# Pair 31's transposes: from TensorE to VectorE's 32x32 blocks, in a graph-attention kernel

## The chip, the cores and the metric

One core of one Trainium2 chip. The metric is the device time of one execution in microseconds. Before the change it is 289.98 us, the median of 3 runs (289.61 to 290.26).

## What is computed

Two graph layers with a residual and a layer norm each, over 64 graphs of 128 nodes and 256 features:

```python
# layer 0, for each graph
q, k = split(X @ Wqk);  v = X @ Wv
agg = adj @ (k * mask)
w   = mask * (q * agg).sum(-1) / 16          # one weight per node
x1  = layernorm(X + softmax(w over nodes)[:, None] * v)
# layer 1, for each graph
query, key, value = x1 @ Wq.T + bq, x1 @ Wk.T + bk, x1 @ Wv.T + bv
e   = adj * exp(query @ key.T)
out = layernorm(x1 + (e / e.sum(-1)) @ value)
```

## The kernel before

Two graphs make a pair; there are 32 pairs, 0 to 31. A slot t of the program works on several pairs at once: it projects pair t+2 and forms its node weights and their softmax, it finishes x1 of pair t+1, it runs layer 1's queries, values and scores for pair t, and it attends and stores for pair t-1 and before. Every engine runs its own queue in the order in which the code lists it, with semaphores between the queues. The slots run from -2 to 29; slot 29 (`DRAIN`, PAIRS - 3) is the last one, and each engine then has a hand-written `drain()` for what is left of pairs 29, 30 and 31. There pair 30 is called `a` and pair 31 `b`.

The softmax over the nodes needs the node weights as a row. VectorE writes them as two columns, `w_col` (128 nodes by 2 graphs), so they have to be transposed into rows, and the softmax's result transposed back into the columns `p_col`, by which VectorE scales the projected values in `sum_x1` (L656). There are two ways, and `by_tensor(pair)` (L30) chooses:

- By TensorE (pairs 0, 1, 2 and 31). `transpose_w` of TensorE (L995) writes the rows to PSUM, VectorE takes their maximum (`row_max`, L818), ScalarE the exponentials and their sum (L597), VectorE inverts the sum (`invert_sum`, L814) and scales the row into `p_row` (L907), TensorE transposes it (`transpose_p`, L1001), and VectorE copies two columns of the result to `p_col` (L660).
- By VectorE (pairs 3 to 30). `transpose_w` of VectorE transposes `w_col` in four blocks of 32x32 (L809), the maximum and the exponentials follow, ScalarE scales the row (`scale_row`, L493) between the two halves of the z copy (L485), and VectorE transposes that row back in four blocks (L912).

Around the change, in slot 29 and behind it: VectorE's `attended` part computes x2 of pair 28 in two halves (L883) and takes its statistics (L646), the first instruction of VectorE's `drain()` is `x1t_lo_a`, the low part of pair 30's transposed x1 (L732), and `sum_x1(31)` (L665) stands behind it. From there runs x1 of pair 31: statistics (L646), variance (L744), the root on GpSimd (L317), the norm on VectorE (L694), TensorE's transposes of x1 (L1076). TensorE's queries and values of pair 30 stand between its score matmuls (L1050) and L1076; the first of them wait for `x1t_lo_a`.

Of the kernel before, what the change touches and what calls it, by code (L numbers as in the profile page):

```python
# [13 lines left out]
PAIRS = GRAPHS // 2  # L14
# [10 lines left out]
FIRST, DRAIN = -2, PAIRS - 3  # L25
# [3 lines left out]

def by_tensor(pair):  # L30

    return pair < 3 or pair == PAIRS - 1


def exists(pair):

    return not isinstance(pair, int) or 0 <= pair < PAIRS


def build(nc, x_pairs, xt_pairs, adjt_pairs, params0, params1, value_bias, out_pairs):  # L40
    ctx = ExitStack()
    with ctx:  # L42
# [140 lines left out]
        def graph(g, width=DIM):  # L183
            return slice(g * width, (g + 1) * width)
# [21 lines left out]
        def w_rows(r):  # L206
            return w_row_ps(r) if by_tensor(r) else w_row[0:2, :]
# [4 lines left out]
        def p_full_ps(r):  # L212
            return yv_ps(r)[:, 1, 0:NODES]
# [230 lines left out]
        def _(act):  # L444
# [94 lines left out]
            def slot(t, r):  # L539
# [59 lines left out]
                if exists(t) and r != 0:  # L599
                    act.wait_ge(z_done, t + 1)  # L600
                    bias_half(z, 0, z_half_copied)
                    if exists(t + 2) and not by_tensor(r + 2):
                        scale_row(t + 2, r + 2)
                    bias_half(z, 1, z_copied)
# [337 lines left out]
        def _(pe):  # L942
# [5 lines left out]
            def split_product(out, parts):  # L948

                for n, (s_hi, s_lo, m_hi, m_lo) in enumerate(parts):  # L950
                    mm = split_half(out, s_hi, s_lo, m_hi, m_lo, n == 0, n == len(parts) - 1)
                return mm

            def aggregate(u, r):

                if r < SPLIT:
                    pe.wait_ge(adjm_done, u + 1)
                    pe.wait_ge(x_loaded[r % 4], transfers4(u, r))
                else:
                    pe.wait_ge(adjm_lo_done, u + 1 - SPLIT)  # L960
                    pe.wait_ge(x_lo_done, u + 1 - SPLIT)
                if exists(u - 1):
                    pe.wait_ge(agg_copied, u)
                for g in range(2):
                    n = graph(g, NODES)
                    if r < SPLIT:
                        mm = nc.tensor.matmul(agg_ps[:, g, :], adjm[r % 2][:, n], x_raw[r % 4][:, graph(g)],  # L967
                                              start=True, stop=True)
                    else:
                        mm = split_product(agg_ps[:, g, :], [(adjm_hi[r % 2][:, n], adjm_lo[r % 2][:, n],  # L970
                                                              x_hi[r % 2][:, graph(g)], x_lo[r % 2][:, graph(g)])])
                mm.then_inc(agg_done, 1)
# [6 lines left out]
            def project(u, r, g):  # L979

                if g == 0:
                    pe.wait_ge(xt_lo_done, u)
                if exists(u - 1) and r > 1:
                    pe.wait_ge(x1_sum_done[g], 1 if r == 2 else u)
                for k in range(HALVES):
                    mm = project_half(u, r, g, k)
                    if r == 2 and g == 0 and k == HALVES - 1:
                        transpose_p(1, 1)
                mm.then_inc(yv_done[g], 1)

            def transpose_w(u, r):

                for g in range(2):
                    pe.wait_ge(w_done[g], u + 1)
                nc.tensor.transpose(w_row_ps(r), w_col[:, 0:2], ident[:, :]).then_inc(w_row_done, 1)  # L995

            def transpose_p(u, r):

                pe.wait_ge(ident_ready, 1)
                pe.wait_ge(p_row_done, u + 1)  # L1000
                nc.tensor.transpose(p_full_ps(r), p_row[:, :], ident[:, :]).then_inc(p_col_done, 1)  # L1001
# [19 lines left out]
            def transpose_x1(out, r):  # L1021
                for g in range(2):
                    if r == 0 and g == 1:
                        pe.wait_ge(x1_done, 1)
                    for k in range(HALVES):
                        c = g * DIM + k * 128
                        mm = nc.tensor.transpose(out[:, k, g, :], x1[r % 2][:, c:c + 128], ident[:, :])  # L1027
                mm.then_inc(x1t_done, 1)

            def queries(hi, lo, weighted=None):  # L1030
                for m in range(HALVES):
                    if m == 1 and weighted:
                        transpose_w(*weighted)
                    c = slice(m * 128, (m + 1) * 128)
                    mm = split_product(z_ps[:, m, :], [(
                        at_hi[:, k, c], at_lo[:, k, c], hi[:, k, :, :].rearrange("p g n -> p (g n)"),
                        lo[:, k, :, :].rearrange("p g n -> p (g n)")) for k in range(HALVES)])
                mm.then_inc(z_done, 1)

            def values(hi, lo, g):  # L1040
                return split_product(val_ps[:, g, 0:VAL_COLS], [(
                    hi[:, k, g, :], lo[:, k, g, :], wv1_hi[:, k, :], wv1_lo[:, k, :]) for k in range(HALVES)])

            def scores(u, out, zs, xs):
                pe.wait_ge(z_half_copied, u + 1)
                for k in range(HALVES):
                    if k == 1:
                        pe.wait_ge(z_copied, u + 1)
                    for g in range(2):
                        mm = nc.tensor.matmul(out[:, g, :], zs[:, k, graph(g, NODES)], xs[:, k, g, :],  # L1050
                                              start=(k == 0), stop=(k == HALVES - 1))
                mm.then_inc(score_done, 1)
# [57 lines left out]
            def transpose_next(t, r):  # L1110
                if r == -1:
                    pe.wait_ge(first_half_normed, 1)
                    pe.wait_ge(biases_ready, 1)
                else:
                    pe.wait_ge(x1_done, t + 2)
                    pe.wait_ge(z_copied, t + 1)
                transpose_x1(x1t_ps, r + 1)

            def slot(t, r):
                if exists(t + 2):  # L1120
                    if r > 0:
                        aggregate(t + 2, r + 2)
                    project(t + 2, r + 2, 0)
                if exists(t + 2):
                    project(t + 2, r + 2, 1)
                if exists(t - 1):

                    pe.wait_ge(edge_lo_done, t)
                    pe.wait_ge(val_lo_done, t)
                    for g in range(2):  # L1130
                        n = graph(g, NODES)
                        mm = split_product(sum_ps[:, g, 0:VAL_COLS], [(edge_hi[:, n], edge_lo[:, n],
                                                                       val_hi[:, g, :], val_lo[:, g, :])])
                    mm.then_inc(sum_done, 1)
                if exists(t):

                    pe.wait_ge(x1t_lo_done, t + 1)
                    if r == 0:
                        pe.wait_ge(at_lo_done, HALVES + 1)
                        pe.wait_ge(wv1_lo_done, 1)  # L1140
                        pe.wait_ge(biases_ready, 1)
                    queries(x1t_hi, x1t_lo, (t + 2, r + 2) if r > 0 and by_tensor(r + 2) else None)
                if r == DRAIN:
                    pe.wait_ge(x1_done, t + 2)
                    pe.wait_ge(agg_copied, PAIRS)
                    transpose_x1(x1t_drain_ps, r + 1)
                if exists(t):

                    values(x1t_hi, x1t_lo, 0)
                    if r == 0:  # L1150
                        transpose_w(2, 2)
                    values(x1t_hi, x1t_lo, 1).then_inc(val_done, 1)
                    if r == DRAIN:
                        transpose_p(t + 2, r + 2)

                    if exists(t - 1):
                        pe.wait_ge(x2_done, t)
                    else:
                        for g in range(2):
                            pe.wait_ge(x1_sum_done[g], 2)  # L1160
                    scores(t, score_ps, z, x1t)
                if r != DRAIN:
                    if by_tensor(r + 2):
                        transpose_p(t + 2, r + 2)
                    transpose_next(t, r)
# [39 lines left out]
            transpose_w(1, 1)  # L1205
            transpose_next(-1, -1)
            slots(pe, slot, 0)
            drain()

# [32 lines left out]
```

## Time and profile before

| | |
|---|---|
| median of 3 runs | 289.98 us |
| profiled execution | 290.11 us |
| its span, first to last instruction | 288.3 us |
| mean granted TensorE clock | 0.995 |
| TensorE busy | 281.0 us (97%) |
| VectorE busy | 250.2 us (87%) |
| ScalarE busy | 248.5 us (86%) |
| GpSimd busy | 216.3 us (75%) |

The profile is one execution. Its span is 1.8 us shorter than its time: what lies around the first and the last instruction. Slot 29 and the drain fill the stretch from about 261 us to the end. PE is TensorE's matmuls, PEld its weight loads, DVE VectorE, ACT ScalarE, POOL GpSimd. A matmul of PE is shown longer than the distance to the next one, since they are pipelined; starts tell the queue's pace better than durations.

### The profile page before, as it was taken

The page shows a single profiled execution, that of the slowest core. Times are in us where ns is not written, and L with a number is a line of the kernel's source. Part 1 is how long each engine was busy: PE and PEld are TensorE (multiplying, and loading weights), DVE is VectorE, ACT ScalarE, POOL GpSimd, SP SyncE. Part 2 cuts the span into 40 slices and gives each one's busy share as a digit, 9 for nine tenths or more (in the row PEclk, how much of TensorE's full clock was granted, in tenths as well). Part 3 has the DMA queues.
Part 4 walks back from the last instruction along what each step waited for, and adds up shares of the span by engine and source line. Part 5 has one row for each costly group of instructions (what it writes and reads, how often), then busy time and mean ns, then how long its engine had stood idle before and what let it go on. Part 6 is the DMA issues. An engine that isn't in the chain of part 4 may idle for free.

```text
span 288.3 us, 7134 instructions
## 1 busy us (share of the span) xinstructions
PE 281.0 (97%) x1956; PEld 261.6 (91%) x1956; DVE 250.2 (87%) x841; ACT 248.5 (86%) x625; POOL 216.3 (75%) x269
## 2 busy tenths in 40 slices
PE   8999999999999999999999999999999999999991
PEld 7889999999999999999999999999999999999990
DVE  1588999999899999998999998999999989999775
ACT  3445889999999999999999999999999999998763
POOL 1546988788898888789887888988887898877332
PEclk9999999999999999999999999999999999999997
DMA  6930234232344323334433333434233334210112
GB/s 231 338 107 38 91 95 116 89 110 94 111 129 127 118 87 104 98 102 127 127 102 100 108 97 103 127 127 118 89 103 96 105 127 127 91 54 28 48 39 110
DMA packets 19166, 31.27 MB, mean 108 GB/s; under 512 B 2128, under 2 KB 6608, under 8 KB 19152
## 3 DMA queue, kind: packets, MB, share of 16 engines
q1 hardware_dynamic: 19152, 31.11, 35.0%
q8 instruction: 6, 0.10, 0.1%
q14 instruction: 8, 0.07, 0.1%
HBM read 22.71 MB, written 8.39 MB: 108 GB/s over the span
## 4 chain that ended last, share of the span: by engine, by line
PE 94%; DMA 2%; DVE 1%; issue 1%; ACT 0%; POOL 0%; SPq 0%; POOLq 0%; DVEq 0%; ACTq 0%
PE ps L944 25%; PE ps L945 25%; PE ps L946 25%; PE ps L1050 10%; PE ps L1027 5%; DMA p<-params 2%; PE ps L967 1%; PE ps L1183 1%; PE ps L1055 1%; PE ps L1006 1%; PE ps L1190 0%; DVE x L684 0%; POOLq L42 0%; POOL rstd L317 0%; PE ps L1012 0%
## 5 line engine op out<-in xcount | busy, mean ns | idle before, releaser
L944 PE MATMUL ps<-w_hi,xt_hi 128*128 128x512 f32 x124 | 49.1, 396 | 0.0
L945 PE MATMUL ps<-w_lo,xt_hi 128*128 128x512 f32 x124 | 48.6, 392 | 0.0
L946 PE MATMUL ps<-w_hi,xt_lo 128*128 128x512 f32 x124 | 48.5, 391 | 0.0
L377 POOL TENSOR_TENSOR edge_lo<-edge,edge_hi 128x256 fp32r<-128x256 f32 x29 | 21.5, 741 | 32.3 <-ACT edge_hi L558 32.3
L310 POOL TENSOR_TENSOR x1b<-x,bv_all 128x512 f32<-128x512 f32 x31 | 39.9, 1289 | 3.0 <-DVE x L883 2.1
L364 POOL TENSOR_TENSOR xt_lo<-xt_raw,xt_hi 128x512 fp32r<-128x512 f32 x30 | 38.4, 1281 | 1.6 <-ACT xt_hi L450 1.6
L388 POOL TENSOR_TENSOR rstd<-var_eps,minus_half 128x4 f32<-128x4 f32 x31 | 31.6, 1019 | 9.3 <-DVE var_eps L855 9.2
L371 POOL TENSOR_TENSOR x_lo<-x_raw,x_hi 128x512 fp32r<-128x512 f32 x28 | 36.2, 1294 | 0.0
L944 PE MATMUL ps<-wv_hi,x1t_hi 128*128 128x258 f32 x124 | 35.7, 288 | 0.0
L640 DVE CUSTOM_DVE_ANT_0 agg<-ps,agg,adjt 128x256 f32<-128x256 f32 x64 | 30.4, 479 | 5.6 <-issue 3.8
L946 PE MATMUL ps<-wv_hi,x1t_lo 128*128 128x258 f32 x124 | 35.2, 284 | 0.0
L945 PE MATMUL ps<-wv_lo,x1t_hi 128*128 128x258 f32 x124 | 35.2, 284 | 0.0
L944 PE MATMUL ps<-x1t_hi,at_hi 128*128 128x256 f32 x124 | 35.2, 284 | 0.0
L945 PE MATMUL ps<-x1t_lo,at_hi 128*128 128x256 f32 x124 | 34.9, 282 | 0.0
L946 PE MATMUL ps<-x1t_hi,at_lo 128*128 128x256 f32 x124 | 34.8, 280 | 0.0
L468 ACT ACTIVATE x<-x,shift,rstd 128x256 f32<-128x256 f32 x62 | 34.2, 605 | 0.3 <-POOL shift L322 0.3
L468 ACT ACTIVATE x<-x_sum,shift,rstd 128x256 f32<-128x256 f32 x58 | 31.7, 594 | 2.4 <-POOL shift L391 2.4
L1050 PE MATMUL ps<-x1t,z 128*128 128x128 f32 x240 | 31.7, 275 | 0.0
L665 DVE SCALAR_TENSOR_TENSOR x_sum<-ps,p_col,x_raw 128x256 f32<-128x256 f32 x64 | 28.0, 480 | 2.8
L485 ACT ACTIVATE z<-ps,z_bias 128x256 f32<-128x256 f32 x62 | 27.7, 453 | 2.5 <-PE ps L946 2.5
L883 DVE SCALAR_TENSOR_TENSOR x<-ps,den_inv,x1b 128x256 f32<-128x256 f32 x58 | 26.8, 468 | 3.5
L1050 PEld LDWEIGHTS ps<-x1t,z 128*128 128x128 f32 x240 | 29.6, 192 | 0.0
(173 smaller groups left out, 912.1 us busy)
## 6 DMA issues: line engine op xcount, KB each, us to landing
xt_raw<-xt_pairs SPq DMA_DIRECT2D x32, 256.0 KB, 2.7
x_raw<-x_pairs SPq DMA_DIRECT2D x32, 256.0 KB, 2.7
out_pairs<-x SPq DMA_DIRECT2D x31, 256.0 KB, 2.0
adjt<-adjt_pairs SPq DMA_DIRECT2D x32, 129.0 KB, 2.1
p<-params SPq DMA_DIRECT2D x1, 770.0 KB, 6.6
p<-params SPq DMA_DIRECT2D x1, 512.0 KB, 3.8
p<-params SPq DMA_DIRECT2D x1, 256.0 KB, 4.8
out_pairs<-x SPq DMA_DIRECT2D x2, 128.0 KB, 1.8
```

What stands on the lines that cost most here:

```text
L310: nc.gpsimd.tensor_tensor(to[:, :].rearrange("p (g d) -> p g d", g=2), x1[r % 2][:, :].rearrange("p (g d) -> p g d", g=2), bv_all[:, :].un ...
L364: nc.gpsimd.tensor_tensor(xt_lo[r % 2][:, :, :, :].rearrange("p t g n -> p (t g n)"), xt_raw[r % 2][:, :], xt_hi[r % 2][:, :, :, :].rearra ...
L371: nc.gpsimd.tensor_tensor(x_lo[r % 2][:, :], x_raw[r % 4][:, :], x_hi[r % 2][:, :].bitcast(F32), ALU.subtract).then_inc(x_lo_done, 1)
L388: nc.gpsimd.tensor_tensor(rstd[r % 2][:, :, :], var_eps[:, :, :], minus_half[:, :, :], ALU.pow)\
L468: last = nc.scalar.activation(out[:, graph(g)], in_[:, graph(g)], ACT.Identity, bias=shift[r % 2][:, layer, g:g + 1], scale=rstd[r % 2][:, ...
L485: nc.scalar.activation(to[:, m, :], z_ps[:, m, :], ACT.Identity, bias=z_bias[:, m:m + 1]).then_inc(done, 1)
L640: nc.vector.tensor_tensor_reduce(agg[:, g, :], y_ps(r)[:, g, :], agg[:, g, :], adjt[r % 4][:, PAIR_N + g:PAIR_N + g + 1], 0.0, ALU.mult, A ...
L665: nc.vector.scalar_tensor_tensor(out=x1_sum[r % 2][:, graph(g)], in0=v0_ps(r)[:, g, :], scalar=p_col[:, g:g + 1], in1=x_raw[r % 4][:, grap ...
L944: nc.tensor.matmul(out, s_hi, m_hi, start=first, stop=False)
L945: nc.tensor.matmul(out, s_hi, m_lo, start=False, stop=False)
L946: return nc.tensor.matmul(out, s_lo, m_hi, start=False, stop=last)
L1050: mm = nc.tensor.matmul(out[:, g, :], zs[:, k, graph(g, NODES)], xs[:, k, g, :], start=(k == 0), stop=(k == HALVES - 1))
```

## The change

`by_tensor` is true for pairs 0, 1 and 2 alone, and TensorE's `transpose_p` in slot 29 is gone; its `transpose_w` of that slot goes by the same condition. Pair 31 so takes the way of pairs 3 to 30.

```diff
 def by_tensor(pair):
-    return pair < 3 or pair == PAIRS - 1
+    return pair < 3
...
                     values(x1t_hi, x1t_lo, 1).then_inc(val_done, 1)
-                    if r == DRAIN:
-                        transpose_p(t + 2, r + 2)
```

In VectorE's queue, slot 29, from the second accumulator read of pair 31's weights (`w_col`) on; `x_0` is x2 of pair 28:

```order
 L640 ISA w_col 128x1
-L872 RECIPROCAL den_inv<-ps 128x2
-L883 SCALAR_TENSOR_TENSOR x_0<-ps,den_inv,x1b 128x256
-L818 TENSOR_REDUCE neg_max<-ps 2x1
+L809 STREAM_TRANSPOSE w_row<-w_col 32x32 x4
+L818 TENSOR_REDUCE neg_max<-w_row 2x1
+L872 RECIPROCAL den_inv<-ps 128x2
+L883 SCALAR_TENSOR_TENSOR x_0<-ps,den_inv,x1b 128x256
+L814 RECIPROCAL inv_sum<-exp_sum 2x1
 L883 SCALAR_TENSOR_TENSOR x_0<-ps,den_inv,x1b 128x256
```

Four block transposes come in, the maximum moves ahead of the first half of x2, and the inversion of the sum ahead of its second half.

Next in the same queue, to `sum_x1(31)`, across the border between the slot and the drain:

```order
 L646 BN_STATS stats<-x_0 128x6
-L814 RECIPROCAL inv_sum<-exp_sum 2x1
-L907 TENSOR_SCALAR p_row<-ps,inv_sum 2x128
+L912 STREAM_TRANSPOSE p_col<-ps 32x32 x4
 L732 TENSOR_TENSOR x1t_lo_a<-ps,x1t_hi_a 128x512
-L660 COPY p_col<-ps 128x2
 L665 SCALAR_TENSOR_TENSOR x_sum<-ps,p_col,x_raw 128x256 x2
```

Three short instructions go, and four block transposes stand ahead of `x1t_lo_a`.

In ScalarE's queue, slot 29, between the norm of pair 30 and the high part of its transposed x1:

```order
-L597 ACTIVATE ps,exp_sum<-ps,neg_max 2x128
-L485 ACTIVATE z<-ps,z_bias 128x256 x2
+L597 ACTIVATE ps,exp_sum<-w_row,neg_max 2x128
+L485 ACTIVATE z<-ps,z_bias 128x256
+L493 ACTIVATE ps<-ps,inv_sum 2x128
+L485 ACTIVATE z<-ps,z_bias 128x256
 L607 CAST x1t_hi_a<-ps 128x512
```

The row scaling stands between the two halves of the z copy. TensorE's queue loses one L995 and one L1001 and nothing in it moves; GpSimd's and the DMA queue keep their order.

## Rows read from the trace of the kernel before

**Rows 1.** The page's chain that ended last, shares of the span by engine.
```profile
PE 94%; DMA 2%; DVE 1%; issue 1%; ACT 0%; POOL 0%; SPq 0%; POOLq 0%; DVEq 0%; ACTq 0%
```

**Rows 2.** Timeline of weight loads: start us, duration us, engine, line, operation, [idle before].
```profile
269.70 0.14 PEld L1001 LDWEIGHTS ps<-ident,p_row 128*128 128x128 f32 x1
269.81 0.97 PEld L1050 LDWEIGHTS ps<-x1t,z 128*128 128x128 f32 x8
270.70 0.19 PEld L944 LDWEIGHTS ps<-x1t_hi_a,at_hi 128*128 128x128 f32 x1
...
273.45 0.19 PEld L946 LDWEIGHTS ps<-wv_hi,x1t_lo_a 128*128 128x128 f32 x1
273.79 0.46 PEld L1076 LDWEIGHTS ps<-ident,x 128*128 128x128 f32 x4 [0.16 <-issue]
```

**Rows 3.** Timeline of VectorE, slot 29 and the drain's start.
```profile
266.37 0.08 DVE L640 DVE_READ_ACCUMULATOR2_ANT w_col<- 128x1 f32 x1
...
267.41 0.28 DVE L818 TENSOR_REDUCE neg_max<-ps 2x1 f32<-2x128 f32 x1
267.62 0.46 DVE L883 SCALAR_TENSOR_TENSOR x<-ps,den_inv,x1b 128x256 f32<-128x256 f32 x1
268.11 0.71 DVE L646 BATCH_NORM_STATS2 stats<-x 128x6 f32<-128x512 f32 x1
268.74 0.13 DVE L814 RECIPROCAL inv_sum<-exp_sum 2x1 f32<-2x1 f32 x1
268.91 0.34 DVE L907 TENSOR_SCALAR p_row<-ps,inv_sum 2x128 f32<-2x128 f32 x1
269.54 0.69 DVE L732 TENSOR_TENSOR x1t_lo_a<-ps,x1t_hi_a 128x512 fp32r<-128x512 f32 x1 [0.29 <-ACT x1t_hi_a L607]
270.15 0.15 DVE L660 COPY p_col<-ps 128x2 f32<-128x2 f32 x1
270.40 0.88 DVE L665 SCALAR_TENSOR_TENSOR x_sum<-ps,p_col,x_raw 128x256 f32<-128x256 f32 x2
...
273.26 0.73 DVE L694 TENSOR_SCALAR x<-x_sum,neg_mean,rstd 128x256 f32<-128x256 f32 x2 [0.90 <-POOL rstd L317]
```

**Rows 4.** Timeline of GpSimd in the drain.
```profile
272.45 1.38 POOL L317 TENSOR_TENSOR rstd<-var_eps,minus_half 128x2 f32<-128x2 f32 x2 [2.93 <-DVE var_eps L744]
```

**Rows 5.** Timeline of VectorE, slot 28, where pair 30 goes by blocks.
```profile
257.96 0.09 DVE L640 DVE_READ_ACCUMULATOR2_ANT w_col<- 128x1 f32 x1
258.14 0.84 DVE L809 STREAM_TRANSPOSE w_row<-w_col 32x32 f32<-32x32 f32 x4
259.01 0.27 DVE L818 TENSOR_REDUCE neg_max<-w_row 2x1 f32<-2x128 f32 x1
259.22 0.15 DVE L872 RECIPROCAL den_inv<-ps 128x2 f32<-128x2 f32 x1
...
259.89 0.14 DVE L814 RECIPROCAL inv_sum<-exp_sum 2x1 f32<-2x1 f32 x1
259.96 0.45 DVE L883 SCALAR_TENSOR_TENSOR x<-ps,den_inv,x1b 128x256 f32<-128x256 f32 x1
260.42 0.87 DVE L912 STREAM_TRANSPOSE p_col<-ps 32x32 f32<-32x32 f32 x4
261.39 0.88 DVE L665 SCALAR_TENSOR_TENSOR x_sum<-ps,p_col,x_raw 128x256 f32<-128x256 f32 x2
```

**Rows 6.** Timeline of ScalarE, slot 28 (first two) and slot 29.
```profile
260.08 0.31 ACT L493 ACTIVATE ps<-ps,inv_sum 2x128 f32<-2x128 f32 x1
260.33 0.45 ACT L485 ACTIVATE z<-ps,z_bias 128x256 f32<-128x256 f32 x1
...
268.12 0.84 ACT L485 ACTIVATE z<-ps,z_bias 128x256 f32<-128x256 f32 x2
268.85 0.59 ACT L607 CAST x1t_hi_a<-ps 128x512 fp32r<-128x512 f32 x1
```

**Rows 7.** Stretch 281 to 283 us: busy time of each engine, granted clock, DMA.
```profile
281.00:283.00 2.00, 1.38 (x5) 0.59 (x4) 1.81 (x9) 1.61 (x4) 0.87 (x2) 1.00 0.02 4
```

## The prediction, made before the changed kernel ran

> **What bounds the kernel now.** I read the chain that ended last, then TensorE's weight loads, then VectorE's timeline in the last slot and the drain, then the same stretch one slot earlier. The chain gives TensorE 94% of the span [rows 1]. So two things can be worth something: time in TensorE's queue, and a delay of whatever TensorE waits for. The change touches one pair of 32, in the last slot, and so the question is who sets the time there.
>
> The place to look is L1076, the transposes of pair 31's x1. Up to there TensorE works without a break, and behind it stands everything that is left of pair 31. The load ahead of it (L946) starts at 273.45 and L1076's first at 273.79, a step of 0.34 [rows 2]. An identity load that waits for nothing follows sooner: L1001's successor starts 269.81 - 269.70 = 0.11 behind it [rows 2]. The engine sat idle for 0.16, put down to "issue", which names nobody [rows 2]. But L1076 waits by its code for the first half of L694, VectorE's norm of pair 31, which started at 273.26 [rows 3], and for two ScalarE copies. The norm had waited 0.90 for GpSimd's root [rows 3], and the root 2.93 for VectorE's variance [rows 4], which hangs on the statistics of x_sum, L665, started at 270.40 [rows 3]. So I read: from 270.40 on the time runs L665, statistics, root, norm, L1076. TensorE alone would have been ready some 0.34 - 0.11 = 0.23 sooner. The chain view follows TensorE through this place because the wait is short; it is still VectorE's.
>
> Behind L1076, the attention matmuls (L1055), the halves of x1t, the queries of pair 31 and the rest all follow from L694 or from L1076. A shift of L665 therefore moves all of it, and the end, by the same amount, if nothing in between was late for another reason.
>
> **The change step by step, on VectorE.** All times are those of the profiled execution. Up to the second accumulator read at 266.37 nothing differs [rows 3]. From there I lay the steps of slot 28, where pair 30 already goes by blocks [rows 5], over slot 29:
> - read to L809: 258.14 - 257.96 = 0.18, so 266.55.
> - L809 x4 to L818: 259.01 - 258.14 = 0.87, so the maximum at 267.42. Before it stood at 267.41 [rows 3]: the first four transposes cost the maximum nothing, as they fill the time in which TensorE's transpose was made and x2's first half was done. That first half now comes later.
> - L818 to L872: 0.21, so 267.63; L872 to L814: 259.89 - 259.22 = 0.67, so 268.30; L814 to the second L883: 0.07, so 268.37. Before, that half started at 267.62 [rows 3]. VectorE is 0.75 late here.
> - second L883 to the statistics: 268.11 - 267.62 = 0.49 [rows 3], so 268.86.
> - statistics to what is next: 268.74 - 268.11 = 0.63 [rows 3], so L912 starts at 269.49. L814 (0.17 to the next start) and L907 are gone from here [rows 3].
> - L912 x4: 0.87 from the first start to the last end [rows 5], or some 0.22 from start to start. The next instruction does not wait for them by a semaphore, so I let it start one such step behind the last, at 0.88 to 0.89: `x1t_lo_a` at 270.38. Before: 269.54, where it had waited 0.29 for ScalarE [rows 3]. That wait is used up, 0.84 of delay is left.
> - `x1t_lo_a` to its successor: 270.15 - 269.54 = 0.61 [rows 3], so L665 at 270.99, since L660 (0.25 to the next start) is gone. Before: 270.40.
>
> The sum is +0.59 at L665. As a balance of the same terms: in come 0.87 + 0.89 of transposes with their 0.10 of lead; out go L907 with L814's place there, L660, and the idle 0.29 [rows 3].
>
> Is the sum complete? The new L912 waits for the scaled row. The maximum starts as before, so the exponentials do too, and the z copy's first half still starts at 268.12 [rows 6]. Halves are 0.36 apart, so L493 is due at 268.49; the inverted sum is there at 268.30 + 0.14 = 268.44 by the steps above, just in time. L493 takes 0.31 and is done at 268.80, 0.7 ahead of L912 at 269.49. It holds ScalarE's next one back by 260.33 - 260.08 = 0.25 [rows 6], so `x1t_hi_a` comes at 269.10 instead of 268.85 and ends at 269.69, again 0.7 ahead of `x1t_lo_a` at 270.38. Both new terms on ScalarE cost nothing; the cover is that VectorE has become later than they are. If VectorE were faster there by 0.7, they would show.
>
> **On TensorE.** L995 and L1001 go. L1001's place is 0.11 [rows 2]; I take the same for L995, so 0.22 in all, and this is between 0 and 0.22 of gain only if TensorE is what is late. It is not: its score matmuls L1050 start 0.22 sooner, and then the queries of pair 30, which began at 270.70 with no wait [rows 2], find `x1t_lo_a` ending at 270.38 + 0.69 = 271.07. From the end of a VectorE instruction to TensorE's start I have no clean row here and take 0.05 to 0.15. So TensorE stands idle for roughly 0.65 and starts 0.4 to 0.5 later than before. Its last value load then falls near 273.9, and L1076 is due at 273.79 + 0.59 = 274.38. VectorE remains the late one, more than before.
>
> **Bounds.** The one term that no row shows is what an unrelated instruction waits for behind the last L912. If it could start while the last block is still finishing, as the inversion does behind the statistics (0.63 behind a start of 0.71, so 0.08 before its end [rows 3]), the step is 0.80 and the sum +0.51. If it needed what L665 needs in slot 28, 261.39 - 260.42 = 0.97 [rows 5], the sum is +0.68. I take 0.89, because the blocks themselves show no overlap: four of them fill 0.87 [rows 5].
>
> VectorE's page of the Trainium skill (VectorE: DVE Perf Modes, "Two Vector instructions with no wait between them") says that an instruction which starts in another group of 32 partitions than the last one did is held until all earlier ones have finished. Block transposes that walk over 32 partitions at a time would be held by it, and `x1t_lo_a`, which starts at partition 0, behind the last one too. By that rule it is the upper of the two readings, +0.59; without it +0.51. The rows of the blocks agree with it.
>
> The profiled execution took 290.11, with the change 290.70. It stood 0.13 above the median of its runs; +0.59 on 289.98 is 290.57. A kernel like this can be told from no change from about 0.2% on, which is 0.58 us. The forecast sits on that line.
>
> **Rivals.**
> - *TensorE sets the end after all* (the other side). The gap ahead of L1076 is put down to "issue" and the chain never leaves TensorE there [rows 1, 2]. If L1076 and what follows were not held by VectorE, and the queries of pair 30 had room too, only the two removed transposes count: -0.22, 289.76. It decides if L694 had 0.6 of slack against L1076. Against it: a step of 0.34 where 0.11 is normal, and a norm that itself ended its wait at 273.26.
> - The same page of the Trainium skill ("The three transpose paths" and "Rules for kernel authors") calls VectorE's block transpose the fastest for 32x32 and gives it the shorter time. That speaks for this rival. The rows here speak the other way: 0.11 in TensorE's queue against 0.87 in VectorE's.
> - *The delay reaches the end by TensorE's queue alone.* If x_sum's way had hidden slack (a late ScalarE copy, say) and only the late queries counted, it is 0.5 minus the 0.23 that TensorE had to spare: about +0.3, 290.27. Against it: root and norm waited in the rows for exactly this way.
> - *More than the sum.* TensorE's new gap could bring its granted clock down from 2.4 to 1.2 GHz; the 24 matmuls of pair 30, which took from 270.70 to 273.45 [rows 2], would take twice as long, 2.75 more, so some 293.3. Against it: between 281 and 283 us the engine was busy for 1.38 of 2.00 and the clock stayed 1.00 [rows 7]. A second form of it, the row wait of 0.97, gives +0.68 (290.66).
>
> **How the numbers follow.** The forecast with its bounds of +0.51 to +0.68: 0.80. TensorE sets the end: 0.08. TensorE's queue alone: 0.08. More than the sum: 0.04. Within the forecast a little over half lies above 0.58, so slower is 0.46 + 0.04 = 0.50; the same is 0.34 + 0.08 = 0.42; faster 0.08. The runs before spread by 0.33 around their median, so I set the range from 290.15 to 291.05: it holds the forecast with the runs' spread and the +0.3 case, and leaves out the first rival and the clock.
>
> **What would show it right or wrong.** In the new profile: the maximum at 267.4 as before; L665 at 270.9 to 271.1; TensorE idle for about half a microsecond ahead of pair 30's first query; L1076 later by what L665 is later, and the last store too. It is wrong if L665 is late and L1076 is not, if `x1t_lo_a` or L912 shows a wait for ScalarE, or if the slots before 29 differ at all.

## The result

The changed kernel takes 290.62 us, the median of 21 runs (290.2 to 291.3), the kernel before 290.08 us in 21 runs beside it (289.45 to 290.62). The ratio is 1.0026 with a 95% interval of 1.002 to 1.0032: slower by 0.75 us, 0.58 to 0.93. The medians alone differ by 0.54. The forecast was 290.57, with 0.50 for slower and 0.42 for the same and the line between them at 1.002. The ratio lies on the slower side, the lower end of its interval on the line itself, and the difference of the medians just under it: the kernel is slower than before beyond the noise, but on which side of 0.2% it falls is as open as the forecast had it.

Two executions differ by some tenths of a microsecond in how soon the first loads land, and the difference stays to the end. So I count times of the last slot from one event that stands ahead of every edit in that slot: the end of the slot's weight products, VectorE's second read of the accumulator, called R here. It is at 266.37 in before [rows 3] and at 266.37 after; over the ten profiles it lies between 265.49 and 266.54.

VectorE in the profile of the changed kernel (timeline: start us, duration us, engine, line, operation, tiles, shapes):

```profile
266.37 0.08 DVE L640 DVE_READ_ACCUMULATOR2_ANT w_col<- 128x1 f32 x1
266.54 0.84 DVE L809 STREAM_TRANSPOSE w_row<-w_col 32x32 f32<-32x32 f32 x4
267.42 0.27 DVE L818 TENSOR_REDUCE neg_max<-w_row 2x1 f32<-2x128 f32 x1
...
268.31 0.14 DVE L814 RECIPROCAL inv_sum<-exp_sum 2x1 f32<-2x1 f32 x1
268.37 0.45 DVE L883 SCALAR_TENSOR_TENSOR x<-ps,den_inv,x1b 128x256 f32<-128x256 f32 x1
268.86 0.71 DVE L646 BATCH_NORM_STATS2 stats<-x 128x6 f32<-128x512 f32 x1
269.49 0.85 DVE L912 STREAM_TRANSPOSE p_col<-ps 32x32 f32<-32x32 f32 x4
270.38 0.69 DVE L732 TENSOR_TENSOR x1t_lo_a<-ps,x1t_hi_a 128x512 fp32r<-128x512 f32 x1
270.98 0.86 DVE L665 SCALAR_TENSOR_TENSOR x_sum<-ps,p_col,x_raw 128x256 f32<-128x256 f32 x2
...
273.84 0.74 DVE L694 TENSOR_SCALAR x<-x_sum,neg_mean,rstd 128x256 f32<-128x256 f32 x2 [0.90 <-POOL rstd L317]
...
285.76 0.73 DVE L801 TENSOR_SCALAR x<-x,neg_mean,rstd 128x256 f32<-128x256 f32 x2 [0.81 <-POOL rstd L317]
```

These answer to [rows 3]. The maximum is where it was (267.41), the second half of x2 is 0.75 late (267.62), `x1t_lo_a` 0.84 (269.54) and without its wait for ScalarE, x_sum 0.58 (270.40), the norm 0.58 (273.26). The last instruction on VectorE, the norm of pair 31's output, is 0.56 late against its place in before:

```profile
285.20 0.74 DVE L801 TENSOR_SCALAR x<-x,neg_mean,rstd 128x256 f32<-128x256 f32 x2 [0.81 <-POOL rstd L317]
```

So from x_sum to the end 0.02 is lost of the 0.58. The instruction behind the norm, VectorE's edge weights of pair 29 (L671), is 0.58 late too. It needs ScalarE's exponentials of pair 29 (L475), which are 0.41 late. Before:

```profile
273.17 0.63 ACT L475 ACTIVATE exp_s<-ps,score_bias 128x128 f32<-128x128 f32 x2
273.91 0.42 DVE L671 TENSOR_TENSOR edge<-exp_s,adjt 128x256 f32<-128x256 f32 x1
```

and after:

```profile
273.58 0.62 ACT L475 ACTIVATE exp_s<-ps,score_bias 128x128 f32<-128x128 f32 x2
274.49 0.42 DVE L671 TENSOR_TENSOR edge<-exp_s,adjt 128x256 f32<-128x256 f32 x1
```

TensorE's weight loads after, which answer to [rows 2]:

```profile
269.59 0.98 PEld L1050 LDWEIGHTS ps<-x1t,z 128*128 128x128 f32 x8
271.12 0.19 PEld L944 LDWEIGHTS ps<-x1t_hi_a,at_hi 128*128 128x128 f32 x1 [0.55 <-DVE x1t_lo_a L732]
...
273.86 0.19 PEld L946 LDWEIGHTS ps<-wv_hi,x1t_lo_a 128*128 128x128 f32 x1
274.37 0.46 PEld L1076 LDWEIGHTS ps<-ident,x 128*128 128x128 f32 x4 [0.32 <-issue]
```

The score matmuls start 0.22 sooner (269.81 before), which is what two transposes took; then comes a wait of 0.55 that before had not (the granted clock stays 1.00 through it, from 270.4 to 273.8), and the wait ahead of L1076 has grown from 0.16 to 0.32. ScalarE, which answers to [rows 6]:

```profile
268.13 0.45 ACT L485 ACTIVATE z<-ps,z_bias 128x256 f32<-128x256 f32 x1
268.48 0.32 ACT L493 ACTIVATE ps<-ps,inv_sum 2x128 f32<-2x128 f32 x1
...
269.10 0.56 ACT L607 CAST x1t_hi_a<-ps 128x512 fp32r<-128x512 f32 x1
```

The row is scaled by 268.80, 0.7 ahead of the blocks; nobody waits for it. Of the chain that ended last, these are two of the 27 pieces between 269.5 and 275.5 us (start us, us, what):

```profile
270.98 0.86 DVE x_sum L665 x2
...
273.84 0.43 DVE x L694
```

In before this view ran along TensorE through the whole stretch, in 32 pieces, of which none is VectorE's. Now that the waits are longer, it names VectorE. The page's chain after gives PE 2%, DVE 3%: these shares cover a small part of the span, so this chain says nothing of the kernel as a whole. The timelines of the two kernels agree from 30 us to R, TensorE's weight loads within 0.01 us and the other engines within 0.04.

### The profile page after: what moved, and what is told of

It is laid out like the page before. It is cut to its first block and busy times, and to the rows that moved or that the text cites. A ratio compares the mean times of both kernels' runs of the same rounds, so it can differ in the third digit from the quotient of the medians.

```text
span 288.9 us, 7135 instructions
## 1 busy us (share of the span) xinstructions
PE 281.4 (97%) x1954; PEld 261.9 (91%) x1954; DVE 251.1 (87%) x847; ACT 248.8 (86%) x626; POOL 216.1 (75%) x269
## 5 line engine op out<-in xcount | busy, mean ns | idle before, releaser
L665 DVE SCALAR_TENSOR_TENSOR x_sum<-ps,p_col,x_raw 128x256 f32<-128x256 f32 x64 | 28.0, 479 | 2.7
```

The costliest lines, as they stand in the source:

```text
L665: nc.vector.scalar_tensor_tensor(out=x1_sum[r % 2][:, graph(g)], in0=v0_ps(r)[:, g, :], scalar=p_col[:, g:g + 1], in1=x_raw[r % 4][:, grap ...
```

## The experiments

Each kernel ran beside the kernel before, which took 290.01 us (24 runs) beside the first four and 290.08 (21 runs) beside the others. Line numbers shift by a few with the edits. A table of all, with distances from R in microseconds; "L1076" is its first load, "edge" the start of VectorE's edge weights of pair 29 (L671), "end" the start of the last norm (L801):

| kernel | x_sum | L1076 | edge | end | end against before | timed ratio, 95% interval |
|---|---|---|---|---|---|---|
| before | 4.03 | 7.42 | 7.54 | 18.83 | | |
| changed | 4.61 | 8.00 | 8.12 | 19.39 | +0.56 | 1.0026, 1.002 to 1.0032 |
| rows by blocks only | 4.35 | 7.75 | 7.87 | 19.14 | +0.31 | 1.002, 1.001 to 1.0029 |
| columns by blocks only | 4.43 | 7.82 | 7.94 | 19.20 | +0.37 | 1.002, 1.0011 to 1.0029 |
| blocks once more | 5.50 | 8.89 | 9.01 | 20.28 | +1.45 | 1.0037, 1.0023 to 1.0051 |
| TensorE's transposes kept | 4.62 | 8.00 | 8.12 | 19.39 | +0.56 | 1.0033, 1.0021 to 1.0045 |
| statistics later | 4.01 | 7.39 | 7.52 | 18.78 | -0.05 | 0.9996, 0.9987 to 1.0005 |
| sum first | 4.08 | 8.48 | 8.73 | 20.01 | +1.18 | 1.0051, 1.0037 to 1.0065 |
| TensorE delayed | 4.03 | 7.66 | 7.91 | 19.18 | +0.35 | 1.0014, 1.0005 to 1.0023 |

The table shows what the end hangs on. It comes 11.26 to 11.29 behind the edge weights in every kernel, while from L1076 to the end it is 11.38 to 11.41 in seven of them and 11.52 or 11.53 in the last two. The edge weights start 0.65 or 0.66 behind the norm of pair 31, or 0.66 behind the exponentials of pair 29, whichever comes later; only in the last two is it the exponentials. L1076 hangs on the same norm, and so it moves with the end as long as the norm is the later one.

The theory that the experiments test: VectorE's queue from R to x_sum(31) sets the end of both kernels, one to one. The rivals: TensorE's queue does, or the delay comes by it alone, or ScalarE's new scaling costs it.

**Rows by blocks only.** The kernel before with the weight rows by VectorE, the columns by TensorE as before.

```diff
+def rows_by_tensor(pair):
+    return pair < 3
...
-                    if not by_tensor(r + 2):
+                    if not rows_by_tensor(r + 2):
                         transpose_w(t + 2, r + 2)
                         row_max(t + 2, r + 2)
```

> Half of the change: pair 31's weight rows by VectorE's blocks, its columns still by TensorE. Theory (VectorE's queue up to x_sum of pair 31 sets the end): from the rows of before, the maximum at 267.42, second half of x2 at 268.31, statistics 268.80, the row scaling 269.60, x1t_lo_a 269.88, the p_col copy 270.49, x_sum (L670 here) at 270.74 instead of 270.40, so +0.34 on the time, L1076's successor line 0.34 later. Rival (TensorE's queue alone carries the delay): its transpose of the row waits until about 270.05 instead of 269.81, 0.24 late, all of it eaten by the 0.23 that TensorE had to spare: 0.0.

```profile
266.54 0.08 DVE L645 DVE_READ_ACCUMULATOR2_ANT w_col<- 128x1 f32 x1
...
270.24 0.14 PEld L1006 LDWEIGHTS ps<-ident,p_row 128*128 128x128 f32 x1 [0.41 <-issue]
...
270.89 0.88 DVE L670 SCALAR_TENSOR_TENSOR x_sum<-ps,p_col,x_raw 128x256 f32<-128x256 f32 x2
```

x_sum is 4.35 behind R instead of 4.03: +0.32 where +0.34 was expected, and the end follows with +0.31. TensorE waited 0.41 ahead of its transpose of the row, by its code for the scaled row, and still it was not what counted for L1076, which moved by 0.33. The rival had TensorE only 0.24 late; in fact the queries of pair 30 came 0.38 late, and less the 0.20 that TensorE had to spare (see the delayed kernel below) that is 0.18, still too little. For the end this experiment alone can't tell the two apart: the exponentials at 7.18 would have let the edge weights start at 7.84, and the norm let them at 7.87. The time agrees (+0.58, 0.29 to 0.84), though it can't tell 0.31 from the full change.

**Columns by blocks only.** The changed kernel with the rows by TensorE again, the row scaled on ScalarE, the columns by blocks.

```diff
+def rows_by_tensor(pair):
+    return pair < 3 or pair == PAIRS - 1
...
+                        if rows_by_tensor(r + 2):
+                            invert_sum(t + 2)
                         dve.wait_ge(p_row_done, t + 3)
```

> The other half: the rows still by TensorE, pair 31's columns by blocks and its row scaling on ScalarE. Theory (VectorE's queue): inverted sum at 268.74 as before, ScalarE's scaling ends at about 269.3, blocks from 269.35, x1t_lo_a 270.24, x_sum at 270.84: +0.44. Together with the other half's +0.34 this is more than the +0.58 of both, because each half alone keeps one wait that the whole change drops. Rival (TensorE's queue alone): queries of pair 30 begin at about 271.05 instead of 270.70, minus 0.23 to spare: +0.1.

```profile
266.14 0.08 DVE L645 DVE_READ_ACCUMULATOR2_ANT w_col<- 128x1 f32 x1
...
269.03 0.87 DVE L919 STREAM_TRANSPOSE p_col<-ps 32x32 f32<-32x32 f32 x4 [0.39 <-ACT ps L498]
...
270.57 0.87 DVE L670 SCALAR_TENSOR_TENSOR x_sum<-ps,p_col,x_raw 128x256 f32<-128x256 f32 x2
```

+0.40 at x_sum, +0.37 at the end; +0.44 was expected. Here the blocks do wait for ScalarE, 0.39, since the sum is inverted later. Through the exponentials, at 7.03, the edge weights could have started at 7.69 and not at the 7.94 at which they did, so here it is VectorE's queue alone. The halves give 0.31 and 0.37, together 0.68, and the whole change 0.56. The rows show one reason: this half keeps a wait, 0.39, that the whole drops.

**Blocks once more.** Four more block transposes on VectorE, into a spare tile, behind the real ones.

```diff
                         block.then_inc(p_copied, 1)
+                        if r == DRAIN:
+                            for b in range(0, NODES, BLOCK):
+                                nc.vector.transpose(spare[b:b + BLOCK, :], p_row_ps(r + 2)[:, b:b + BLOCK])
```

> The changed kernel with four more block transposes on VectorE, of the same row into a spare tile, right behind the real ones. Theory (VectorE's queue, one to one): x_sum at 270.98 + 0.88 = 271.86, and the end 0.88 later than the changed kernel, 1.46 above before. Rival (TensorE's queue alone): the queries of pair 30 late by the same 0.88, which gives also +0.88; the two part in what holds L1076, whose wait must then name or follow the norm (theory) or follow the last value load by 0.11 (rival).

```profile
265.49 0.08 DVE L641 DVE_READ_ACCUMULATOR2_ANT w_col<- 128x1 f32 x1
...
269.50 0.87 DVE L917 STREAM_TRANSPOSE spare<-ps 32x32 f32<-32x32 f32 x4
270.39 0.69 DVE L733 TENSOR_TENSOR x1t_lo_a<-ps,x1t_hi_a 128x512 fp32r<-128x512 f32 x1
270.99 0.87 DVE L666 SCALAR_TENSOR_TENSOR x_sum<-ps,p_col,x_raw 128x256 f32<-128x256 f32 x2
...
274.38 0.46 PEld L1080 LDWEIGHTS ps<-ident,x 128*128 128x128 f32 x4 [0.31 <-issue]
```

x_sum comes 5.50 behind R, 0.89 more than in the changed kernel, and the end 0.89 more. The engine still waits ahead of L1076 (L1080 here), 0.31, so VectorE holds it. R itself came 0.88 earlier in this execution than in before's. Of this 0.34 is there by 31 us, as in the other profiles; the rest builds up evenly over the slots, to 0.62 at 157 us and 0.83 at 250 us. In no other kernel does it grow. So something in this version, which also has one tile more (`spare`), makes each slot some 0.02 shorter; what it is stays open. Of the 1.45 in the last slot the time should then show, by an estimate from these rows, 1.45 - 0.54 = 0.91; timed it is 1.07 (0.67 to 1.48).

**TensorE's transposes kept.** The changed kernel with both transposes back in TensorE's queue, results unused.

```diff
                     if m == 1 and weighted:
                         transpose_w(*weighted)
+                    if m == 1 and again:
+                        for g in range(2):
+                            pe.wait_ge(w_done[g], PAIRS)
+                        nc.tensor.transpose(ps[0:2, 3, 0:128], w_col[:, 0:2], ident[:, :])
...
+                    if r == DRAIN:
+                        nc.tensor.transpose(ps[:, 1, 0:128], p_row[:, :], ident[:, :])
                     scores(t, score_ps, z, x1t)
```

> The changed kernel with TensorE's two transposes of that pair put back at their old places, their results unused. Theory: TensorE waits for x1t_lo_a anyway, from 270.6 to 271.12; two transposes of 0.11 each shorten that wait and move nothing, 0.0 against the changed kernel, +0.6 against before. Rival (TensorE sets the end): +0.22 against the changed kernel, +0.8 against before.

```profile
265.87 0.08 DVE L640 DVE_READ_ACCUMULATOR2_ANT w_col<- 128x1 f32 x1
...
270.62 0.19 PEld L944 LDWEIGHTS ps<-x1t_hi_a,at_hi 128*128 128x128 f32 x1 [0.34 <-DVE x1t_lo_a L732]
...
273.87 0.46 PEld L1080 LDWEIGHTS ps<-ident,x 128*128 128x128 f32 x4 [0.32 <-issue]
```

The wait for `x1t_lo_a` falls from 0.55 to 0.34, so the two transposes took 0.21 out of an idle stretch; L1076 and the end are where the changed kernel has them, 8.00 and 19.39 behind R. What the change takes from TensorE is worth nothing. It is the trace that shows this: the timed +0.96 (0.61 to 1.31) holds the rival's 0.8 as well and can't decide.

**Statistics later.** The changed kernel with the statistics of x2 of pair 28 and layer 1's variance moved from ahead of the blocks into VectorE's wait for the root. GpSimd waits once more for the second variance.

```diff
-                if r == DRAIN:
-                    dve.wait_ge(x2_done, t)
-                    both_stats(1, x2[(r - 1) % 4]).then_inc(stats2_done, 1)
...
+                variance(0)
+                dve.wait_ge(x2_done, DRAIN)
+                both_stats(1, x2[(DRAIN - 1) % 4]).then_inc(stats2_done, 1)
+                dve.wait_ge(stats2_done, DRAIN)
+                variance(1)
```

> The changed kernel with one piece of VectorE's work taken off the way to x_sum of pair 31: the statistics of x2 of pair 28 (0.63) and layer 1's variance run in the 0.90 in which VectorE waits for the root. Theory (VectorE's queue up to x_sum): counted from the second accumulator read, the blocks wait for ScalarE's row and start at 2.50 instead of 3.12, x_sum at 4.00 instead of 4.61 (before: 4.03), so the end is 0.6 earlier than the changed kernel's and 0.0 against before. Rival (the cost of the change lies in something else, ScalarE's scaling or the block transposes as such): it stays 0.3 to 0.6 above before.

```profile
266.03 0.08 DVE L641 DVE_READ_ACCUMULATOR2_ANT w_col<- 128x1 f32 x1
...
268.50 0.87 DVE L911 STREAM_TRANSPOSE p_col<-ps 32x32 f32<-32x32 f32 x4
...
270.04 0.87 DVE L666 SCALAR_TENSOR_TENSOR x_sum<-ps,p_col,x_raw 128x256 f32<-128x256 f32 x2
...
271.90 0.70 DVE L647 BATCH_NORM_STATS2 stats<-x 128x6 f32<-128x512 f32 x1
...
272.89 0.73 DVE L695 TENSOR_SCALAR x<-x_sum,neg_mean,rstd 128x256 f32<-128x256 f32 x2
```

The blocks start 2.47 behind R instead of 3.12, x_sum at 4.01, and the end is 0.61 sooner than in the changed kernel and 0.05 sooner than in before. The norm no longer shows a wait: the statistics fill it. With the eight block transposes and ScalarE's scaling still in the kernel the whole cost is gone, so what costs is VectorE's time in front of x_sum, and neither of them as such. Timed it is the same as before, 289.91 against 290.08. The same move was not tried on the kernel before; an estimate from its rows is that it would gain nothing there, since `x1t_lo_a` waited for ScalarE [rows 3] and could start no sooner.

**Sum first.** The changed kernel with `sum_x1(31)` ahead of `x1t_lo_a`.

```diff
+                sum_x1(b, b)
                 dve.wait_ge(edge_lo_done, DRAIN)
                 dve.wait_ge(x1t_hi_done, a + 1)
                 nc.vector.tensor_tensor(x1t_lo_a[:, :, :, :], x1t_drain_ps, x1t_hi_a[:, :, :, :].bitcast(F32),
                                         ALU.subtract).then_inc(x1t_lo_done, 1)
-                sum_x1(b, b)
```

> The changed kernel with x_sum of pair 31 ahead of x1t_lo_a in VectorE's queue. x_sum starts about 0.5 earlier, x1t_lo_a 0.87 later, the statistics of x_sum 0.1 later. Theory (the later of the two ways into L1076 sets it, VectorE's or TensorE's): TensorE's last value load moves 0.87, past the norm, and L1076 comes 0.47 later than in the changed kernel, +0.5 on it and +1.05 on before. Rival (only x_sum's way counts): +0.1 on the changed kernel, +0.7 on before.

```profile
266.49 0.08 DVE L640 DVE_READ_ACCUMULATOR2_ANT w_col<- 128x1 f32 x1
...
272.10 0.19 PEld L944 LDWEIGHTS ps<-x1t_hi_a,at_hi 128*128 128x128 f32 x1 [1.41 <-DVE x1t_lo_a L733]
...
274.84 0.19 PEld L946 LDWEIGHTS ps<-wv_hi,x1t_lo_a 128*128 128x128 f32 x1
274.97 0.46 PEld L1076 LDWEIGHTS ps<-ident,x 128*128 128x128 f32 x4
275.22 0.42 DVE L671 TENSOR_TENSOR edge<-exp_s,adjt 128x256 f32<-128x256 f32 x1 [0.52 <-ACT exp_s L475]
```

L1076 now follows the last value load by 0.13 and without a wait: TensorE sets it, 0.48 later than in the changed kernel (0.47 expected), though x_sum came 0.53 sooner. The norm is where the changed kernel has it, 7.47 behind R, since the statistics of x_sum now stand behind `x1t_lo_a`. So both ways into L1076 are real, and the later one counts. The end, however, is 0.62 later, 0.14 more than L1076. The last row says where from: VectorE's edge weights of pair 29 waited 0.52 for ScalarE's exponentials, which stand behind the z copy of pair 30 and so behind its queries. That is a third way, which none of the expectations had. Timed it is 1.48 later than before (1.07 to 1.89), above the rival's 0.7.

**TensorE delayed.** The kernel before with four more transposes ahead of the queries of pair 30.

```diff
                 pe.wait_ge(x1t_lo_done, a + 1)
+                pe.wait_ge(z_copied, DRAIN + 1)
+                for _ in range(4):
+                    nc.tensor.transpose(ps[0:2, 0, 0:128], w_col[:, 0:2], ident[:, :])
                 queries(x1t_hi_a, x1t_lo_a)
```

> The kernel before with four more transposes on TensorE, 0.11 each, ahead of the queries of pair 30, results unused. Theory (TensorE had 0.23 to spare ahead of L1076): 0.44 - 0.23 = +0.21 on before, L1076 then follows the last value load by 0.11. Rival (TensorE sets the end of before): +0.44. Rival (it has plenty of room): 0.0.

```profile
266.22 0.08 DVE L640 DVE_READ_ACCUMULATOR2_ANT w_col<- 128x1 f32 x1
...
270.56 0.41 PEld L1063 LDWEIGHTS ps<-ident,w_col 128*2 128x2 f32 x4
271.00 0.19 PEld L944 LDWEIGHTS ps<-x1t_hi_a,at_hi 128*128 128x128 f32 x1
...
273.88 0.47 PEld L1079 LDWEIGHTS ps<-ident,x 128*128 128x128 f32 x4
274.13 0.42 DVE L671 TENSOR_TENSOR edge<-exp_s,adjt 128x256 f32<-128x256 f32 x1 [0.27 <-ACT exp_s L475]
274.61 0.73 PEld L1055 LDWEIGHTS ps<-val,edge 128*128 128x128 f32 x4 [0.26 <-DVE edge L671]
```

Of 0.44 put into TensorE's queue, 0.24 reached L1076: in before the engine had 0.20 to spare there (0.23 was read from the rows). The end moved by 0.35, again more than the expected 0.21, and by the same third way: the edge weights waited 0.27 for ScalarE and the attention matmuls 0.26 for them. On this way in before the room was only 0.08: exponentials at 6.80 let the edge weights start at 7.46, and the norm held them to 7.54. The timed +0.41 (0.15 to 0.67) holds both the theory's 0.21 and the first rival's 0.44; the rows decide. In the changed kernel the queries are 0.42 late and this way stays hidden, since the norm in front of the edge weights is 0.58 late itself: the exponentials, 7.21 behind R, would let them start at 7.87, and they start at 8.12.

**Blocks backwards.** The changed kernel with the four blocks of pair 31's columns written from partition 96 down to 0, seen in one profiled execution.

```diff
-                        for b in range(0, NODES, BLOCK):
+                        blocks = range(0, NODES, BLOCK)
+                        for b in reversed(blocks) if r == DRAIN else blocks:
```

> The changed kernel with the four blocks of pair 31's columns written from partition 96 down to 0. If an instruction that starts in another group of 32 partitions than the one before is held until that one has finished: the first block starts about 0.1 later behind the statistics (0.73 instead of 0.63), and x1t_lo_a less than 0.89 behind the first block, 0.80 to 0.85, in sum the same x_sum within 0.05. If there is no such rule: 0.63 and 0.89 as in the changed kernel.

```profile
266.52 0.08 DVE L640 DVE_READ_ACCUMULATOR2_ANT w_col<- 128x1 f32 x1
...
269.02 0.71 DVE L646 BATCH_NORM_STATS2 stats<-x 128x6 f32<-128x512 f32 x1
269.76 0.87 DVE L913 STREAM_TRANSPOSE p_col<-ps 32x32 f32<-32x32 f32 x4
270.57 0.64 DVE L732 TENSOR_TENSOR x1t_lo_a<-ps,x1t_hi_a 128x512 fp32r<-128x512 f32 x1
271.13 0.85 DVE L665 SCALAR_TENSOR_TENSOR x_sum<-ps,p_col,x_raw 128x256 f32<-128x256 f32 x2
```

From the statistics to the first block it is 0.74 instead of 0.63, from the first block to `x1t_lo_a` 0.81 instead of 0.89, and x_sum is 4.61 behind R as in the changed kernel. This is what the page of the Trainium skill (VectorE: DVE Perf Modes, "Two Vector instructions with no wait between them") foretells: the step into another group of 32 partitions is held until the instruction before has finished, 0.71 here, and a step within the group is not.

## Why the prediction was right, step by step

- *The maximum at 267.42 at no cost*: 267.42.
- *The second half of x2 at 268.37, the blocks at 269.49, x1t_lo_a at 270.38, x_sum at 270.99*: 268.37, 269.49, 270.38, 270.98. Laying the steps of slot 28 over slot 29 worked to 0.01 us, because VectorE's queue had no wait left there that slot 28 had not.
- *The one unknown step, 0.88 to 0.89 behind the blocks and not 0.80 or 0.97*: 0.89, and the backwards blocks show why.
- *The balance of the same terms*: it does not add up as it is written. In come 0.87, 0.89 and 0.10, and out go 0.80 (L814 and L907 with the idle 0.29) and 0.25, which leaves 0.81 and not 0.59. The steps are right. What the balance lacks is that from R to the second half of x2 the rest of VectorE's work takes 1.12 instead of 1.25: 0.88 + 0.89 - 0.13 - 0.80 - 0.25 = 0.59.
- *ScalarE's scaling is hidden*: nobody waited for it. With the statistics later the blocks came right behind it, at 2.47 behind R, and still showed no wait.
- *TensorE's gain is worth nothing; the queries begin 0.4 to 0.5 late*: 0.42 late, and putting the transposes back changed nothing.
- *VectorE holds L1076, with 0.23 of room on TensorE*: 0.20 by the delayed kernel. Here lay the risk of the forecast, as the wait was put down to "issue".
- *Behind L1076 stands everything that is left*: this step was not quite right. The end follows the edge weights of pair 29, which stand behind the same norm as L1076 but can also be held by ScalarE's exponentials. For the end TensorE had not 0.23 to spare but 0.08. The forecast did not suffer, since it let L665 move L694 and all behind it, and the norm stayed the later one.
- *The end follows x_sum one to one*: 0.56 of 0.58, and 0.89 of 0.89 when the blocks were doubled.
- *The time*: +0.59 was forecast; timed it is +0.75 (0.58 to 0.93), the difference of the medians is 0.54, and the trace has +0.56, just below the interval. What makes up the rest between 0.56 and 0.75, if it is more than noise, stays open. The forecast lies between them.
- *TensorE's clock in its new gap*: the rival of 293.3 did not come; the granted clock stayed 1.00.
- *The chance of faster, 0.08*: by the forecast's own line it belongs to the same, since -0.22 on 289.98 is less than 0.1%.

One rival was nearer than the prediction had it: the delay by TensorE's queue alone. It was priced at 0.5 - 0.23, about +0.3, by the way into L1076. That way would have given 0.41 - 0.20 = 0.21. By ScalarE's exponentials and the edge weights, which the prediction had not seen, it is 7.87 - 7.54 = 0.33. So the rival's price was near what TensorE's queue would have cost, by luck, and it stayed hidden because VectorE's delay was larger by 0.25.

## What to carry to other kernels

Moving work off the engine that is busy 97% of the span gained nothing, because in the last slot that engine waits for another one: with its two transposes put back only its wait shrank, by 0.21; what an instruction costs at the end of a program is its time in the queue that the last chain goes through, not on the engine that is busiest on average. A short idle before an instruction that is put down to "issue" deserves a look at what its code waits for: here 0.16 of it was VectorE's whole chain. The room that such a gap suggests is only the room at that instruction: 0.20 at L1076 was 0.08 at the end, because TensorE's queue had another way there. And before swapping the method, look for work in front of the critical instruction that can stand in a wait behind it: moving one statistics instruction of 0.63, with its variance, recovered as much as the change had cost.

## What the runs showed of the hardware

The weights transposed by VectorE in four 32x32 blocks took 0.88 of VectorE's queue (1.77 with the way back), against 0.11 each in TensorE's queue for a transpose of the same data. Two VectorE instructions overlapped by 0.06 to 0.08 where the second stayed in the same group of 32 partitions (it started 0.63 behind one of 0.71, and 0.81 behind the first of four blocks of 0.87 in all), and not at all where it changed the group (0.74 behind 0.71, and 0.89 behind the first of four of 0.85 in all). From the end of `x1t_lo_a` to TensorE's first load that waited for it 0.05 passed (270.38 + 0.69 to 271.12).
